# A local attention stage rewritten as one interleaved order of tiles on every engine

## The chip, the cores and the metric

The kernel runs on one core of a Trainium2 chip. The metric is the device time of one execution in microseconds; the time shown for a kernel is the median of its runs. The core has five engines that each work through their own program: TensorE (PE, with its weight loads as PEld), VectorE (DVE), ScalarE (ACT), GpSimd (POOL) and SyncE (SP), which here only issues transfers. They meet through semaphores: an instruction waits until a counter has reached a value, and another one counts it up when it is done.

## The reference, cut to what matters

A tensor x of 4 x 1024 tokens by 128 features is normalised. One branch is a small block attention (16 heads, blocks of 32). The other is two layers of local attention with a feed-forward part; the two are multiplied and added to x. The change touches the local attention only:

```
h = shift_token(x);  q, k, v = split(h @ wqkv, 3)          # 8 heads of 64
q = l2norm(q) * qs;  k = l2norm(k) * ksc
q, k = rotary_xpos(q, k)
# windows of 64 tokens; each sees its own window and the one before it
sim = einsum('bhwid,bhwjd->bhwij', q * 8, [k_prev_window, k_window])
sim = where(mask, -max, sim);  attn = softmax(sim)
out = einsum('bhwij,bhwjd->bhwid', attn, [v_prev_window, v_window])
x = x + out @ wo
```

## The kernel before

All 4096 tokens are kept in SBUF, features on partitions. The local stage of a layer (L = 0, 1) goes over 32 tiles of 128 tokens; `local(n, par)` is one step of it on each engine, and `steps` calls it for n in a row. After it comes the feed-forward part in 8 chunks of 512 tokens, and before the first stage the block attention.

For one tile m the work is this. TensorE projects q, k and v (three matmuls of 512 columns each, the input split into a high and a low half) into banks 0, 1 and 2 of PSUM. ScalarE squares q and k, VectorE sums the squares, and ScalarE makes inverse norms of them (Relu, Ln, Exp: `lognt`, `ss`). VectorE turns q by position (`tA`, `tB`, `qr`) and scales k (`kn`), GpSimd turns k (`kA`, `kB`, `kr`) and multiplies q by its inverse norm (line 1359). TensorE transposes qr and kr into bank 3, ScalarE copies them to `qT` and `kT`. Masks and scores go to banks 4 and 5 in two groups of heads; VectorE takes maxima (line 1130), ScalarE exponentials with their sums (line 880), VectorE the inverse sums, GpSimd multiplies the probabilities by them (line 1348). TensorE transposes the probabilities into bank 6, ScalarE copies them to `pT`. The values product (line 415, `ps<-pT,VB` and `ps<-pT,V`) goes to bank 7, ScalarE copies it to `oT`, the output product `ps<-oT,wo` goes to bank 3, and VectorE adds it to X.

A window also sees the one before it. So transfers on SP's queue carry the last 64 columns of `kT` into the other slot (line 376), and the halves of V, crosswise on partitions, into `VB` (lines 378 and 380). A third kind copies each finished tile of X, the second half of its features one token later, into `XS[1]` for the feed-forward part (lines 348 and 349). SP does this in a strict order, one `back(n, par)` a tile, and each transfer waits for its semaphores at its place. The wait on `xs_dma` at the head of `back` is for the XS copies issued by the step before to have landed; it keeps the counter exact.

The order on every engine is written out by hand in `local`. VectorE splits the input 512 tokens at a time, in every fourth step (`split_into`, lines 968 and 970). ScalarE copies V from bank 2 (line 849).

Of the kernel before, what the change touches and what calls it, by code (L numbers as in the profile page):

```python
# [32 lines left out]
P = 128  # L33
# [45 lines left out]
def build(nc, a, out):  # L79
    with ExitStack() as ctx:  # L80
# [52 lines left out]
        V = sb("V", [P, 2, INNER])  # L133
        VB = sb("VB", [P, 2, INNER])
        ss = sb("ss", [P, 2, 2 * HEADS])
# [99 lines left out]
        l_qk = sem("l_qk")  # L235
        l_v = sem("l_v")
        l_sq = sem("l_sq")
        l_qm = sem("l_qm")
        l_norm = sem("l_norm")
# [6 lines left out]
        l_qn = sem("l_qn")  # L246
        l_kr = sem("l_kr")
        l_tr = sem("l_tr")
        l_tre = sem("l_tre")
# [3 lines left out]
        l_score = sem("l_score")  # L253
        l_max = sem("l_max")
        l_exp = sem("l_exp")
        l_rinv = sem("l_rinv")
        l_prob = sem("l_prob")
        l_pT = sem("l_pT")
        l_pTe = sem("l_pTe")
# [48 lines left out]
        def _(sp):  # L308
# [49 lines left out]
            for L in range(DEPTH):  # L358
# [4 lines left out]

                def back(n, par):
                    nxt = 1 - par
                    base = L * TILES
                    turned, done = held(2 * (base + n + 1)), held(base + n + 1)
                    scored, pv1 = held(2 * (base + n)), held(base + n)
                    copied = held(xs_before_local(L) + 32 * (n - 2))
                    if live(n, -3, TILES):  # L370

                        sp.wait_ge(xs_dma, copied)
                    if live(n, 0, TILES):
                        sp.wait_ge(l_tre, turned)
                        wait(sp, l_score, scored)
                        sp.dma_start(kT[:, nxt, :, 0:WIN], kT[:, par, :, P:P + WIN]).then_inc(k_prev[nxt], 16)
                        sp.wait_ge(l_ve, done)
                        sp.dma_start(VB[64:P, par, :], V[0:64, par, :]).then_inc(v_prev[par], 16)
                        wait(sp, l_o, pv1)
                        sp.dma_start(VB[0:64, nxt, :], V[64:P, par, :]).then_inc(v_prev[nxt], 16)  # L380
                    if live(n, -2, TILES):
                        copy_shifted(XS[1], n - 2, P, x_before_local(L) + n - 1)

                if L == 0:

                    sp.wait_ge(zeros_made, 2)
                    sp.wait_ge(windows_zero, 1)
                    sp.dma_start(kT[:, 0, :, 0:WIN], kT[:, 1, :, P:P + WIN]).then_inc(k_prev[0], 16)
                    sp.dma_start(VB[0:64, 0, :], V[64:P, 1, :]).then_inc(v_prev[0], 16)
                steps(0, TILES + 1, back)  # L390
# [22 lines left out]
        def _(pe):  # L413
# [104 lines left out]
            def layer(L, tail):  # L518
# [6 lines left out]
                def project(c, hi, lo, made):  # L525

                    mm3(ps[:, c, :], hi, lo, wqkv[:, 0, c * INNER:(c + 1) * INNER],
                        wqkv[:, 1, c * INNER:(c + 1) * INNER]).then_inc(made, 1)

                def transposed(n, par, src, ready):  # L530
                    pe.wait_ge(ready, base + n + 1)
                    for c in range(4):
                        last = turn(ps[:, 3, c * P:(c + 1) * P], src[:, par, c * P:(c + 1) * P])
                    last.then_inc(l_tr, 1)

                def local(n, par):
                    nxt = 1 - par
                    now, ahead = [[split[:, (m // TPC) % 2, i, (m % TPC) * P:(m % TPC + 1) * P] for i in range(2)]
                                  for m in (n + 2, n + 1)]
                    if live(n, 2, TILES):  # L540
                        pe.wait_ge(l_split, L * CHUNKS + (n + 2) // TPC + 1)
                        wait(pe, l_qm, base + n + 2)
                        project(0, *now, l_qk)
                    if live(n, 0, TILES):

                        wait(pe, x_new, (x_before_local(L) + n - 2) if not isinstance(n, int) or n > 2 else 0)
                        transposed(n, par, qr, l_qn)

                    def scores():
                        if live(n, 0, TILES):  # L550
                            pe.wait_ge(l_tre, 2 * (base + n + 1))

                            pe.wait_ge(k_prev[par], 16 * ((base + n) // 2 + 1))
                            wait(pe, l_exp, 8 * (base + n))

                            first = 1 if par else live_mask(n)
                            half = [slice(64 * i, 64 * i + 64) for i in range(2)]
                            for w, grp in ((0, 0), (1, 1), (1, 0), (0, 1)):
                                kind = 1 if w else first
                                mm(ps[half[w], 4 + grp, :], ident_bf[half[grp], half[grp]],  # L560
                                   lmask[half[grp], bass.ds(kind * CHUNK, CHUNK)], True, False)
                            for s in range(4):
                                for w, grp in ((0, 0), (1, 1), (1, 0), (0, 1)):
                                    last = mm(ps[half[w], 4 + grp, s * P:(s + 1) * P],
                                              qT[half[grp], par, s, half[w]],
# [893 lines left out]
```

## Time and profile before

| | |
|---|---|
| median of 3 runs | 907.86 us (907.16 to 908.72) |
| profiled execution | 909.96 us, its span 908.2 us |
| TensorE busy | 800.1 us (88%) |
| VectorE busy | 664.4 us (73%) |
| ScalarE busy | 654.3 us (72%) |
| GpSimd busy | 523.9 us (58%) |
| chain that ended last | PE 56%, ACT 17%, DVE 16%, issue 7% |
| transfers | 48.24 MB, under 512 B 40410 of 64704 packets |

The span is the time from the first to the last instruction of the profiled execution. Busy time counts only working instructions, so an engine that waits on a semaphore is not busy. The chain goes back from the last instruction, at each step to what released it; it passes through an engine also where that engine waits for others in turn. Times within the span are microseconds from its start. The "granted clock" is the part of TensorE's full clock that it got: 1.00 is 2.4 GHz, 0.50 is 1.2 GHz.

### The profile page before, as it was taken

What the parts mean: (1) busy time and instruction counts of PE and PEld (TensorE: products, weight loads), DVE (VectorE), ACT (ScalarE), POOL (GpSimd) and SP (SyncE); (2) the same over time, 40 slices, a digit from 0 to 9 for tenths busy, and PEclk for the clock granted to TensorE, in tenths of its full rate; (3) what the DMA queues carried; (4) which work ended last, traced back from release to release, by engine and by line L of the source; (5) the groups of instructions that cost most, each with busy time, mean ns of one, the idle gap of its engine ahead of it and who ended that gap; (6) DMA issues with size and microseconds to landing.
All of it is one profiled execution on the core that took longest, in us unless ns stands there. A gap on an engine that the chain in (4) does not pass through costs nothing.

```text
span 908.2 us, 26049 instructions
## 1 busy us (share of the span) xinstructions
PE 800.1 (88%) x9848; PEld 610.5 (67%) x9848; DVE 664.4 (73%) x1347; ACT 654.3 (72%) x2053; POOL 523.9 (58%) x521
## 2 busy tenths in 40 slices
PE   4779999779999999999989887999999999988985
PEld 1458778557777778777756545777877777775652
DVE  1577998677887787877457767778787788745765
ACT  2337777479899899889743337989988998974463
POOL 0363333078888888888511017888888888951100
PEclk8899999889999999999999998999999999999997
DMA  9110001012222222222201121222222222222001
GB/s 308 44 45 3 4 4 41 3 47 55 57 57 63 55 58 55 60 57 63 51 18 24 29 63 37 64 53 58 57 61 56 62 52 58 58 51 100 1 36 58
DMA packets 64704, 48.24 MB, mean 53 GB/s; under 512 B 40410, under 2 KB 50948, under 8 KB 64068
## 3 DMA queue, kind: packets, MB, share of 16 engines
q1 hardware_dynamic: 64580, 46.57, 19.9%
q8 instruction: 80, 1.31, 0.6%
q14 instruction: 44, 0.36, 0.1%
HBM read 10.63 MB, written 2.10 MB: 14 GB/s over the span
## 4 chain that ended last, share of the span: by engine, by line
PE 56%; ACT 17%; DVE 16%; issue 7%; POOL 1%; DMA 1%; SPq 1%; DVEq 0%; ACTq 0%; POOLq 0%
PE ps L415 47%; PE ps L425 9%; ACT prob L880 6%; DVE nmax L1130 3%; ACT sq L822 3%; DVE nt L1158 2%; ACT V L849 2%; ACT oT L831 2%; DVE split L970 2%; ACT kT L856 1%; ACT pT L826 1%; DVE prob L1217 1%; DVE split L968 1%; DMA awo<-in_awo 1%; ACT qT L841 1%
## 5 line engine op out<-in xcount | busy, mean ns | idle before, releaser
L880 ACT ACTIVATE prob<-ps,nmax 128x128 f32<-128x128 f32 x512 | 181.8, 374 | 36.7 <-DVE nmax L1130 36.7
L415 PE MATMUL ps<-wqkv,split 128*128 128x512 f32 x576 | 188.2, 438 | 14.2 <-DVE split L970 10.1
L1348 POOL TENSOR_TENSOR prob<-prob,rinv 128x512 f32<-128x512 f32 x128 | 133.9, 1046 | 88.4 <-DVE rinv L1116 45.8
L415 PEld LDWEIGHTS ps<-wqkv,split 128*128 128x128 f32 x576 | 97.5, 195 | 33.5 <-DVE split L970 10.2
L1130 DVE TENSOR_REDUCE nmax<-ps 128x4 f32<-128x512 f32 x128 | 83.6, 686 | 48.3 <-PE ps L415 48.3
L425 PE MATMUL ps<-ident,prob 128*128 128x128 f32 x640 | 98.3, 276 | 13.9 <-POOL prob L1348 13.1
L880 ACT ACTIVATION_READ_ACCUMULATOR prob<-ps,nmax 128x1 f32 x512 | 109.0, 213 | 0.0
L1359 POOL TENSOR_TENSOR qr<-qr,ss 128x512 f32<-128x512 f32 x64 | 66.9, 1046 | 53.7 <-DVE qr L1142 53.7
L425 PEld LDWEIGHTS ps<-ident,prob 128*128 128x128 f32 x640 | 76.2, 142 | 28.3 <-POOL prob L1348 17.4
L415 PE MATMUL ps<-oT,wo 128*128 128x128 f32 x512 | 73.9, 287 | 22.0 <-ACT oT L831 22.0
L826 ACT ACTIVATE pT<-ps 128x512 f32<-128x512 f32 x128 | 80.0, 625 | 10.7 <-PE ps L425 9.1
L415 PE MATMUL ps<-split,w 128*128 128x512 f32 (+1 forms) x288 | 81.4, 427 | 6.6 <-DVE prob L1217 6.3
L415 PEld LDWEIGHTS ps<-oT,wo 128*128 128x128 f32 x512 | 62.1, 191 | 37.3 <-ACT oT L831 36.3
L822 ACT ACTIVATE sq<-ps 128x512 f32<-128x512 f32 x128 | 81.8, 640 | 5.1 <-PE ps L415 5.0
L1370 POOL TENSOR_TENSOR kr<-kA,kB 128x512 f32<-128x512 f32 x64 | 82.4, 1287 | 5.0
L1364 POOL TENSOR_TENSOR kA<-kn,lrot 128x512 f32<-128x512 f32 x64 | 81.8, 1278 | 0.0
L1313 POOL TENSOR_TENSOR qr<-ident,rstd 128x512 f32<-128x512 f32 x16 | 16.6, 1042 | 99.1 <-DVE rstd L962 96.0
L415 PEld LDWEIGHTS ps<-split,w 128*128 128x128 f32 (+1 forms) x288 | 50.4, 180 | 31.1 <-DVE prob L1217 10.1
L1330 POOL TENSOR_TENSOR prob<-D,hmask 128x512 f32<-128x512 f32 x32 | 35.1, 1097 | 59.5 <-PE ps L415 59.4
L1142 DVE TENSOR_TENSOR qr<-tA,tB 128x512 f32<-128x512 f32 x64 | 68.6, 1072 | 0.0
L415 PE MATMUL ps<-pT,VB 128*64 128x64 f32 x1024 | 66.3, 228 | 1.5 <-issue 1.5
L415 PE MATMUL ps<-kT,qT 64*64 64x128 f32 x2048 | 66.8, 269 | 0.0
(139 smaller groups left out, 1871.9 us busy)
## 6 DMA issues: line engine op xcount, KB each, us to landing
VB<-V SPq DMA_DIRECT2D x129, 128.0 KB, 2.4
kT<-kT SPq DMA_DIRECT2D x65, 128.0 KB, 2.4
XS<-X SPq DMA_DIRECT2D x32, 128.0 KB, 2.3
XS<-X SPq DMA_DIRECT2D x128, 32.0 KB, 1.9
D<-in_xT SPq DMA_DIRECT2D x8, 256.0 KB, 4.4
XS<-in_xT SPq DMA_DIRECT2D x2, 1024.0 KB, 6.7
out_T<-XS SPq DMA_DIRECT2D x8, 256.0 KB, 2.0
raw<-in_wqkv SPq DMA_DIRECT2D x2, 768.0 KB, 4.4
```

Source lines behind the costliest of these rows:

```text
L415: return nc.tensor.matmul(o, l, r, start=start, stop=stop, skip_group_check=True)
L425: return nc.tensor.matmul(o, i, ident[:], is_transpose=True, start=True, stop=True, skip_group_check=True)
L822: nc.scalar.activation(sq[:, c, :], ps[:, c, :], ACT.Square).then_inc(l_sq, 1)
L826: nc.scalar.activation(pT[:, grp, :], ps[:, 6, :], ACT.Copy).then_inc(l_pTe, 1)
L880: nc.scalar.activation(prob[:, par, grp, s * P:(s + 1) * P], ps[:, 4 + grp, s * P:(s + 1) * P], ACT.Exp, bias=nmax[:, par, grp * 4 + s:grp ...
L1130: v.tensor_reduce(nmax[:, par, 4 * grp:4 * grp + 4], ps[:, 4 + grp, :].rearrange("p (s k) -> p s k", s=4), AX_X, ALU.max, negate=True).the ...
L1142: v.tensor_tensor(qr[:, nxt, :], tA[:], tB[:], ALU.add).then_inc(l_qr, 1)
L1330: g.tensor_tensor(kexp[:, par, :].rearrange("p (b h k) -> p b h k", b=BLKS, h=INGRP), part(kR, n, P).rearrange("p (b k) -> p b k", b=BLKS) ...
L1348: g.tensor_tensor(p4, p4, rinv[:, slot, 4 * grp:4 * grp + 4].unsqueeze(2).broadcast_to([P, 4, P]), ALU.mult).then_inc(l_prob, 1)
L1359: g.tensor_tensor(hd(qr[:, nxt, :]), hd(qr[:, nxt, :]), ss[:, nxt, 0:8].unsqueeze(2).broadcast_to([P, HEADS, HD]), ALU.mult).then_inc(l_qn, 1)
L1364: g.tensor_tensor(hd(kA[:]), hd(kn[:]), row8(2, pos, 0, HD), ALU.mult)
L1370: g.tensor_tensor(kr[:, nxt, :], kA[:], kB[:], ALU.add).then_inc(l_kr, 1)
```

## The change

- The local stage is cut into small functions, one for each operation on a tile, and every engine calls them in a written order in which one step works on tiles from n+4 or n+5 down to n-3. TensorE now does the scores of tile n, the values of tile n-2 and the output of tile n-3 in one step; it did the values of n-1 and the output of n-2.
- Semaphores are split: one for q and one for k, and one for each group of heads.
- q is no longer multiplied by its inverse norm on GpSimd. The exponential takes the inverse norm as its scale, a column of `ss`, and the maxima (now `rawmax`) are multiplied by it in two small VectorE operations a tile.
- The split of the input goes from VectorE, 512 tokens at a time, to GpSimd, 128 tokens at a time (`input_high`, `input_low`).
- V is copied out of PSUM by VectorE instead of ScalarE, and has three slots instead of two.
- On SP, the X tile that is copied to XS in a step is that of n-4, it was n-2; the rest of `back` has its old form.

```diff
-        V = sb("V", [P, 2, INNER])
+        V = sb("V", [P, 3, INNER])
...
                 def back(n, par):
-                    nxt = 1 - par
-                    base = L * TILES
-                    turned, done = held(2 * (base + n + 1)), held(base + n + 1)
-                    scored, pv1 = held(2 * (base + n)), held(base + n)
-                    copied = held(xs_before_local(L) + 32 * (n - 2))
-                    if live(n, -3, TILES):
-
-                        sp.wait_ge(xs_dma, copied)
+                    nxt, done = 1 - par, base + n + 1
+                    if live(n, -5, TILES):
+                        sp.wait_ge(xs_dma, xs_before_local(L) + 32 * (n - 4))
                     if live(n, 0, TILES):
-                        sp.wait_ge(l_tre, turned)
-                        wait(sp, l_score, scored)
+                        sp.wait_ge(l_tk, done)
+                        wait(sp, l_score[1], done - 1)
                         sp.dma_start(kT[:, nxt, :, 0:WIN], kT[:, par, :, P:P + WIN]).then_inc(k_prev[nxt], 16)
                         sp.wait_ge(l_ve, done)
-                        sp.dma_start(VB[64:P, par, :], V[0:64, par, :]).then_inc(v_prev[par], 16)
-                        wait(sp, l_o, pv1)
-                        sp.dma_start(VB[0:64, nxt, :], V[64:P, par, :]).then_inc(v_prev[nxt], 16)
-                    if live(n, -2, TILES):
-                        copy_shifted(XS[1], n - 2, P, x_before_local(L) + n - 1)
+                        sp.dma_start(VB[64:P, par, :], V[0:64, done % 3, :]).then_inc(v_prev[par], 16)
+                        wait(sp, l_o, done - 1)
+                        sp.dma_start(VB[0:64, nxt, :], V[64:P, done % 3, :]).then_inc(v_prev[nxt], 16)
+                    if live(n, -4, TILES):
+                        copy_shifted(XS[1], n - 4, P, x_before_local(L) + n - 3)
...
-                steps(0, TILES + 1, back)
+                steps(0, TILES + 3, back)
...
+                def scores(m):
...
+                        pe.wait_ge(l_tq, base + m + 1)
+                        pe.wait_ge(l_tk, base + m + 1)
+
+                        pe.wait_ge(k_prev[m % 2], 16 * ((base + m) // 2 + 1))
...
+                def values_summed(m):
...
+                        wait(pe, l_oe, base + m)
+                        pe.wait_ge(l_pTe[0], base + m + 1)
+                        pe.wait_ge(l_pTe[1], base + m + 1)
+                        pe.wait_ge(l_ve, base + m + 1)
+                        pe.wait_ge(v_prev[m % 2], 32 * ((base + m) // 2 + 1))
...
+                def local(n, par):
+                    q_projected(n + 3)
+                    scores(n)
+                    probs_turned(n - 2, 1)
+                    k_turned(n + 1)
+                    v_projected(n)
+                    values_summed(n - 2)
+                    output(n - 3)
+                    k_projected(n + 3)
+                    probs_turned(n - 1, 0)
+                    q_turned(n + 2)
...
+                def exponentials(m, grp):
+                    if 0 <= m < TILES:
+                        act.wait_ge(l_max[grp], base + m + 1)
+                        for s in range(4):
+                            col = slice(grp * 4 + s, grp * 4 + s + 1)
+                            nc.scalar.activation(prob[:, m % 2, grp, s * P:(s + 1) * P],
+                                                 ps[:, 4 + grp, s * P:(s + 1) * P], ACT.Exp, bias=nmax[:, m % 2, col],
+                                                 scale=ss[:, (base + m) % 3, 2 * s + grp:2 * s + grp + 1],
+                                                 accum_out=rsum[:, m % 2, col]).then_inc(l_exp[grp], 1)
+
+                def local(n, par):
+                    exponentials(n, 1)
+                    exponentials(n, 0)
+                    probs_copied(n - 1, 0)
+                    k_squared(n + 3)
+                    q_copied(n + 2)
+                    q_squared(n + 4)
+                    o_copied(n - 2)
+                    norm_floor(n + 3)
+                    probs_copied(n - 1, 1)
+                    norm_log(n + 3)
+                    k_copied(n + 2)
+                    norm_inverse(n + 3)
...
+                def v_copied(m):
+                    if 0 <= m < TILES:
+                        dve.wait_ge(l_v, base + m + 1)
+                        wait(dve, l_o, base + m - 2)
+                        if base + m >= 2:
+                            dve.wait_ge(v_prev[m % 2], 32 * ((base + m - 2) // 2 + 1))
+                        v.tensor_copy(V[:, (base + m + 1) % 3, :], ps[:, 2, :]).then_inc(l_ve, 1)
...
+                def scaled_maxima(m, grp):
+                    if 0 <= m < TILES:
+                        dve.wait_ge(l_rawmax[grp], base + m + 1)
+                        v.tensor_tensor(nmax[:, m % 2, 4 * grp:4 * grp + 4], rawmax[:, m % 2, 4 * grp:4 * grp + 4],
+                                        ss[:, (base + m) % 3, grp:HEADS:2], ALU.mult).then_inc(l_max[grp], 1)
...
+                    maxima(n, 1)
+                    q_cos(n + 3)
+                    scaled_maxima(n, 1)
+                    maxima(n, 0)
+                    k_scaled(n + 2)
+                    scaled_maxima(n, 0)
+                    q_sin(n + 3)
+                    added_to_x(n - 3)
+                    v_copied(n)
+                    q_summed(n + 3)
+                    inverse_sums(n, 1)
+                    inverse_sums(n, 0)
+                    q_rotated(n + 3)
+                    k_summed(n + 3)
...
-                        g.tensor_tensor(hd(qr[:, nxt, :]), hd(qr[:, nxt, :]),
-                                        ss[:, nxt, 0:8].unsqueeze(2).broadcast_to([P, HEADS, HD]),
-                                        ALU.mult).then_inc(l_qn, 1)
...
                 def local(n, par):
...
+                    input_low(n + 4)
+                    k_sin(n + 2)
+                    k_cos(n + 2)
+                    k_rotated(n + 2)
+                    normalised(n, 1)
+                    input_high(n + 5)
+                    normalised(n, 0)
```

On TensorE, in the middle of the first local stage, from the masks of one tile on, before. `lmask` are the masks, `kT,qT` the scores, `oT,wo` the output product, `pT,VB` and `pT,V` the values, `wqkv,split` a projection, `ident,...` a set of four transposes.

```order
L415 MATMUL ps<-lmask,ident_bf 64x512 x4
L415 MATMUL ps<-kT,qT 64x128 x16
L415 MATMUL ps<-oT,wo 128x128 x4
L415 MATMUL ps<-pT,VB 64x64 x2
L415 MATMUL ps<-pT,V 64x64 x2
```

And of the changed kernel, from the end of the values of one step to those of the next.

```order
L418 MATMUL ps<-pT,V 64x64 x2
L418 MATMUL ps<-oT,wo 128x128 x4
L418 MATMUL ps<-wqkv,split 128x512 x3
L428 MATMUL ps<-ident,prob 128x128 x4
L428 MATMUL ps<-ident,qr 128x128 x4
L418 MATMUL ps<-wqkv,split 128x512 x3
L418 MATMUL ps<-lmask,ident_bf 64x512 x4
L418 MATMUL ps<-kT,qT 64x128 x16
L428 MATMUL ps<-ident,prob 128x128 x4
L428 MATMUL ps<-ident,kr 128x128 x4
L418 MATMUL ps<-wqkv,split 128x512 x3
L418 MATMUL ps<-pT,VB 64x64 x2
```

The values stood behind the output product, right after the scores; they now stand behind two sets of transposes and V's projection, and belong to tile n-2. The output product follows them.

On SP, the transfers of one tile with their waits, before: the kT window, the two halves of VB, the two halves of XS, and the next kT window.

```order
L376 DMA kT<-kT 128x4x64 [waits l_score,l_tre,xs_dma]
L378 DMA VB<-V 64x512 [waits l_ve]
L380 DMA VB<-V 64x512 [waits l_o]
L348 DMA XS<-X 64x128 [waits x_new]
L349 DMA XS<-X 64x128
L376 DMA kT<-kT 128x4x64 [waits l_score,l_tre,xs_dma]
```

And in the changed kernel.

```order
L379 DMA kT<-kT 128x4x64 [waits l_score1,l_tk,xs_dma]
L381 DMA VB<-V 64x512 [waits l_ve]
L383 DMA VB<-V 64x512 [waits l_o]
L354 DMA XS<-X 64x128 [waits x_new]
L355 DMA XS<-X 64x128
L379 DMA kT<-kT 128x4x64 [waits l_score1,l_tk,xs_dma]
```

The places of the transfers are the same; the waits have new names, and XS takes the tile four back instead of two. `l_o` still counts the values of the tile before the one whose kT window was sent last.

## Rows read from the trace of the kernel before

**Rows 1.** Table by stage, second local stage: us, busy time (count) of each engine.
```profile
549.30:806.60 257.30, 233.62 (x3077) 190.05 (x3080) 199.36 (x375) 231.42 (x829) 214.00 (x215) 0.99 0.24 57
```

**Rows 2.** Timeline, TensorE, scores of first and last tiles: start, us, engine, line, out<-in.
```profile
188.78 0.41 PE L415 MATMUL ps<-lmask,ident_bf 64*64 64x512 bf16 x4
...
445.08 0.41 PE L415 MATMUL ps<-lmask,ident_bf 64*64 64x512 bf16 x4
...
446.33 1.16 PE L415 MATMUL ps<-oT,wo 128*128 128x128 f32 x8
...
549.27 0.53 PE L415 MATMUL ps<-lmask,ident_bf 64*64 64x512 bf16 x4
...
806.55 0.41 PE L415 MATMUL ps<-lmask,ident_bf 64*64 64x512 bf16 x4
```

**Rows 3.** Timeline, TensorE, inside one tile.
```profile
341.51 0.34 PE L415 MATMUL ps<-pT,VB 128*64 128x64 f32 x4
...
342.59 0.97 PE L415 MATMUL ps<-wqkv,split 128*128 128x512 f32 x3
...
343.39 0.60 PE L425 MATMUL ps<-ident,qr 128*128 128x128 f32 x4
...
343.83 0.60 PE L425 MATMUL ps<-ident,prob 128*128 128x128 f32 x4
...
344.18 0.94 PE L415 MATMUL ps<-wqkv,split 128*128 128x512 f32 x3
```

**Rows 4.** Timeline, SP's queue of transfers, same tile.
```profile
342.70 0.46 SPq L380 DMA_DIRECT2D VB<-V  x1
...
343.84 0.60 SPq L349 DMA_DIRECT2D XS<-X  x1
347.14 0.63 SPq L376 DMA_DIRECT2D kT<-kT  x1
```

**Rows 5.** Groups of instructions: shapes, count | busy us, mean ns | idle before.
```profile
L849 ACT ACTIVATE V<-ps 128x512 f32<-128x512 f32 x64 | 41.4, 647 | 0.0
...
L1359 POOL TENSOR_TENSOR qr<-qr,ss 128x512 f32<-128x512 f32 x64 | 66.9, 1046 | 53.7 <-DVE qr L1142 53.7
...
L970 DVE TENSOR_TENSOR split<-XS,split 128x512 fp32r<-128x512 f32 x16 | 23.5, 1470 | 0.6
...
L869 ACT ACTIVATE lognt<-lognt,floor 128x16 f32<-128x16 f32 x64 | 19.0, 297 | 0.3
...
L968 DVE CAST split<-XS 128x512 fp32r<-128x512 f32 x16 | 10.2, 635 | 0.0
...
L876 ACT ACTIVATE ss<-lognt 128x16 f32<-128x16 f32 x64 | 14.3, 223 | 0.1
...
L1170 DVE RECIPROCAL rinv<-rsum 128x4 f32<-128x4 f32 x64 | 11.2, 176 | 25.0 <-ACT prob L880 25.0
```

**Rows 6.** DMA issues: first and last kT copy of 62: count, KB, us to landing.
```profile
kT<-kT SPq DMA_DIRECT2D x1, 128.0 KB, 3.8
...
kT<-kT SPq DMA_DIRECT2D x1, 128.0 KB, 3.3
```

**Rows 7.** Tile XS, 250 to 400 us, its 18 pairs of copies.
```profile
DMA to landing us min/median/max: 1.7/1.9/3.3
```

**Rows 8.** Stretches, TensorE: us, busy (count), granted clock, DMA share, GB/s.
```profile
168.60:170.50 1.90, 0.04 (x1) 1.00 0.00 0
170.70:174.10 3.40, 3.40 (x12) 0.50 0.00 0
...
552.00:559.70 7.70, 5.34 (x87) 1.00 0.09 21
559.70:561.70 2.00, 0.01 (x1) 1.00 0.57 131
563.30:566.60 3.30, 3.11 (x12) 0.50 0.00 0
```

**Rows 9.** Timeline, TensorE, a projection at the lower clock.
```profile
195.92 1.63 PE L415 MATMUL ps<-wqkv,split 128*128 128x512 f32 x3
```

More of the change, by code:

```diff
@@ L536, in local @@
[L536 to L557, printed above, removed]
-                            for w, grp in ((0, 0), (1, 1), (1, 0), (0, 1)):
[L559 to L565, printed above, removed]
-                                              kT[half[grp], par, s, 64 * w:64 * w + P], False, True)
-                                    if s == 3 and w != grp:
-                                        last.then_inc(l_score, 1)
-                    def turned_probs(grp):
-                        if live(n, -1, TILES):
-                            pe.wait_ge(l_prob, 2 * (base + n - 1) + grp + 1)
-                            wait(pe, l_pTe, 2 * (base + n - 1) + grp)
-                            for s in range(4):
-                                last = turn(ps[:, 6, s * P:(s + 1) * P], prob[:, nxt, grp, s * P:(s + 1) * P])
-                            last.then_inc(l_pT, 1)
-                    def output():
-                        if not live(n, 0, TILES):
-                            pe.wait_ge(x_new, x_before_local(L) + n - 2)
-                        pe.wait_ge(l_oe, base + n - 1)
-                        if live(n, 0, TILES):
-                            pe.wait_ge(l_tre, 2 * (base + n + 1))
@@ new lines, in probs_turned, with output @@
+                def probs_turned(m, grp):
+                    if 0 <= m < TILES:
+                        pe.wait_ge(l_prob[grp], base + m + 1)
+                        wait(pe, l_pTe[1 - grp], base + m + grp)
+                        for s in range(4):
+                            last = turn(ps[:, 6, s * P:(s + 1) * P], prob[:, m % 2, grp, s * P:(s + 1) * P])
+                        last.then_inc(l_pT[grp], 1)
+                def output(m):
+                    if 0 <= m < TILES:
+                        if m == 0:
+                            pe.wait_ge(wo_in, 16 * (L + 1))
+                        pe.wait_ge(l_oe, base + m + 1)
+                        if 0 <= m + 4 < TILES:
+                            pe.wait_ge(l_tk, base + m + 4 + 1)
+                        elif 0 <= m + 4 < TILES:
+                            pe.wait_ge(l_tq, base + m + 4 + 1)
+                        elif 0 <= m - 1 < TILES:
+                            pe.wait_ge(x_new, x_before_local(L) + m - 1 + 1)
@@ L682, in layer @@
                 local(TILES, 0)
+                bias_products()
+                local(TILES + 1, 1)
+                local(TILES + 2, 0)
                 variance(2, 2, 0)
@@ L1176, in layer @@
                 if L == 0:
                     dve.wait_ge(xs_dma, xs_before_local(0))
-                    local(-3, 1)
                     a_tile(TILES - 1, 1)
-                    local(-2, 0)
-                    local(-1, 1)
+                    steps(-3, -1, local)
                     dve.wait_ge(a_done, TILES)
@@ L1185, in layer @@
                     dve.wait_ge(xs_dma, xs_before_ffn(L - 1) + 32)
+                    steps(-3, -4, local)
+                    tail(CHUNKS, 0)
                     local(-3, 1)
-                    tail(CHUNKS, 0)
                     local(-2, 0)
@@ L1260, in layer @@
                 ffn_bias(L)
-                add_to_x(TILES - 2)
+                local(TILES + 1, 1)
                 def scaled(j, t):
@@ L1378, in _ @@
+                steps(-5, TILES - 1 + 0, local)
+                pool.wait_ge(l_trq, base + TILES)
                 nb = L * CHUNKS
```

457 lines of the change are left out of this document (243 added, 214 removed).

## The prediction

> **What bounds the kernel now.** I read the table by stage first. One local stage (scores of tile 0 to scores of tile 31) is 257.3 us, in which TensorE is busy 233.6, ScalarE 231.4, GpSimd 214.0 and VectorE 199.4 [rows 1]. Over 31 intervals that is 7.54, 7.47, 6.90 and 6.43 us a tile, against 8.30 that pass. No engine is full, two are close. Second, the timeline of TensorE. The scores of tile 0 start at 188.78 and 549.27, those of tile 31 at 445.08 and 806.55 [rows 2], so the two stages take 256.3 and 257.3 us, 513.6 together, 8.28 a tile. Within one tile the pieces, start to next start, are [rows 2, 3]: masks and scores 1.25 (445.08 to 446.33), values 1.08 (341.51 to 342.59), a projection 0.80 (342.59 to 343.39), a set of four transposes 0.44 (343.39 to 343.83) or 0.35 (343.83 to 344.18), and the output product about 1.1, by its 1.16 whose tail lies under the next. A tile has three projections and four sets of transposes (0.35 twice, 0.40 for k, 0.44): 1.25 + 1.1 + 1.08 + 2.40 + 1.54 = 7.4. The 0.9 us between 7.4 and 8.28 is what a better order could give back. Third, the queue of transfers on SP. Each tile issues, strictly in turn, the copy of kT's window, two halves of VB, and two halves of the shifted residual XS. Today it follows at leisure: after the values of a tile end, near 342.59, the second half of VB goes out at 342.70, the second half of XS at 343.84, and the next kT copy at 347.14 [rows 3, 4]. The scores that read this kT copy start a whole tile later, so nothing waits for it.
>
> **The change part by part.**
>
> V's copy leaves ScalarE, 0.65 us a tile, and becomes a VectorE copy. GpSimd's scaling of q goes, 1.05 a tile. VectorE's split, 1.47 + 0.64 for four tiles, is 0.53 a tile and goes to GpSimd in eighths of that work: two operations on 128 columns, each between 0 and the 1.05 of a 512-column operation, together some 0.9. VectorE gains two products on 128x4, near 0.2 each by its smallest rows [rows 5]. Busy times a tile become: ScalarE 7.47 - 0.65 = 6.8, VectorE 6.43 - 0.53 + 0.65 + 0.4 = 6.95, GpSimd 6.90 - 1.05 + 0.9 = 6.75 (5.9 to 8.0), TensorE unchanged.
>
> The exponential now reads its scale from a column. Nearest rows: a 16-column activation with no column operand is 223 ns, one with a column for its bias 297 [rows 5]. I take the difference, 0.07, for each of eight exponentials: 0.6 a tile (0 to 0.6). ScalarE is then 7.4. The Trainium skill, ScalarE: Activation LUTs, section What ACT_TABLE_LOAD costs, gives about 93 ns for each column operand, 0.74 a tile, and ScalarE 7.6; the trace agrees within 20 ns. It would matter only in the fast rival below.
>
> The order on TensorE is what I price highest. In step n it did scores(n), output(n-2), values(n-1). Now it does scores(n), transposes of probabilities(n-2), transposes of k(n+1), V's projection(n), values(n-2), and only then output, k's projection, two sets of transposes, q's projection and scores(n+1). SP's program kept its form. For the scores of tile n+1 it must issue in order: the second VB half, which waits for values(n-2); XS of tile n-5 in two halves; then, after a wait for exactly these two XS copies to land, the kT copy that scores(n+1) waits for. Before, the same entry waited for values that TensorE had done one whole step earlier. Now they are done inside the step. This closes a loop through two landings: scores(n) start, values(n-2) end, VB, XS, XS landed, kT, kT landed, scores(n+1) start.
>
> Its length: scores 1.25, transposes 0.35 and 0.40, a projection 0.80, values 1.08, together 3.88 on TensorE [rows 2, 3]. To the VB issue 0.11 (342.59 to 342.70). To the second XS issue 1.14 (342.70 to 343.84) [rows 4]. To its landing 1.9, median, up to 3.3 [rows 7]; the kT issue at 347.14 is 3.3 after 343.84, so today's queue already shows this wait once. kT's landing: 37 of the 62 copies of both stages take 2.3 to 2.5, the others 3.0 to 4.6, mean 2.8; first and last stand in [rows 6]. Hand-overs 0.1. Sum 3.88 + 0.11 + 1.14 + 1.9 + 2.8 + 0.1 = 9.93 us a tile. In the 6.05 us from the end of the values TensorE has 1.1 + 0.80 + 0.35 + 0.44 + 0.80 = 3.5 of other work, so it stands idle 2.6 (2.0 where kT lands in 2.3).
>
> The skill's page DMA: Bandwidth & Descriptors, section Anatomy of one DMA, fits a transfer as 2.0 us and its bytes at 436 GB/s. By that kT's 128 KB take 2.3 and an XS half of 32 KB takes 2.1; the loop would be 9.6 always. The trace has the same 2.3 for the usual kT copy but 3 to 4.6 for two in five, and the measurement decides.
>
> For which tiles: the XS copies start with step 4 of SP and the wait for them with step 5, so scores(1) to (5) are free of the loop (the chain without XS is 0.11 + 0.5 + 2.8, about 3.4, against 3.5 of work), and scores(6) to (31) are in it: 26 intervals a stage. For the five free ones I take 8.0, between 7.4 and 8.28.
>
> The clock adds to it. Where TensorE stood idle about 2 us, the granted clock afterwards fell to half (1.2 GHz instead of 2.4) for 3.4 us: idle 168.6 to 170.5, half until 174.1; idle 559.7 to 561.7, half from 563.3 to 566.6 [rows 8]. From the first to the last of these there are five such gaps at full clock, and four were followed by it; after the one at 552.0 the clock held at 1.00 until 559.7 [rows 8]. A projection at half clock shows 1.63 where the usual one is 0.97 [rows 3, 9], so 3.4 us at half clock do the work of 2.0 and lose 1.4. The loop leaves a gap of 2.0 or more before each scores, and the slow stretch would follow on the 3.88 that are in the loop. I take 0.8 x 1.4 = 1.1 a tile (0 to 1.7, the whole stretch doubled): 9.9 + 1.1 = 11.0.
>
> Start and end of a stage: one more step to fill and drain, V's projection 0.80, values 1.08, output 1.1, so 3.0 a stage (0 to 6), 6 in all. The XS copies of the last tiles leave later, but the feed-forward part reads its last chunk many steps on.
>
> Sum: stages 2 x (5 x 8.0 + 26 x 11.0) = 652 against 513.6, plus 138.4; fill and drain 6. The profiled execution took 909.96 (span 908.2, with 1.8 around it); 909.96 + 144.4 = 1054.4. The median of the runs shown is 2.1 below the profiled one, so 1052.
>
> **Rivals.**
>
> Clock holds (A). The loop is there but the clock stays full, as after 552.0. 9.9 a tile: 2 x (40 + 257.4) = 594.8, plus 81.2 and 6, less 2.1: 995. With landings always the shortest (1.9 and 2.3) the loop is 9.4: 969. For it: one gap in five. Against it: four in five, and gaps that come every tile.
>
> The wait for XS costs nothing (B), say because these copies are counted as landed from an earlier step. The kT copy then goes right behind the second XS issue: 3.88 + 0.11 + 1.14 + 0.64 + 2.8 + 0.1 = 8.7, which is 2 x (40 + 226) = 532, and 934 in the end. Against it: the count waited for is that of tile n-5, issued one entry before.
>
> The queue is no bound (C), the side of faster. It holds if the kT copy for scores(n+1) is out before values(n-2) end. Then the tile is the fullest engine, TensorE 7.54 with a little waiting, 7.6, and the split's stall on every fourth tile is gone: 62 x 7.6 = 471, minus 42.4, plus 6, so 871. This is the place where it turns: once the chain from the end of the values to the landing of kT is under 3.5 us, nothing of the queue is seen. It is 6.05 by the rows, nearly double.
>
> GpSimd at its upper bound of 8.0 a tile would hide behind the loop and changes nothing.
>
> **How the numbers follow.** Loop with the clock falling in most tiles 0.62 (own range 1020 to 1090: 11.6 a tile gives 1083); A 0.26; B 0.06; C 0.06. Predicted time 1052. The range leaves out C and B and the rim: 975 to 1090. A measurement of this kernel tells 0.2% from nothing. Faster 0.05 (C), same 0.01, slower 0.94.
>
> **What would show it.** After: SP's waits name TensorE before the second VB half, then XS, in front of the kT issue, in every tile from the fifth or sixth; TensorE idle 2 to 3 us right before the masks of each tile; masks to masks 10 to 11.5 us, but near 8 for the first five tiles; the granted clock at half for 3.4 us in most tiles; busy shares of ScalarE and GpSimd down to about 65%. I am wrong if the kT issue stands in the trace well before the end of the values, or if masks follow each other in under 9 us; wrong only on the clock if the gaps are there and it stays at full speed.

## The result, and the profile after

The changed kernel takes 1054.5 us, median of 4 runs (1048.6 to 1062.1), beside 907.5 us for the kernel before (4 runs, 907.1 to 908.7). The ratio is 1.162, with a 95% interval of 1.155 to 1.170. The profiled execution took 1054.97 us, span 1053.2.

First the page of the changed kernel: busy time of each engine, TensorE's granted clock in 40 slices, and the chain that ended last by engine.

```profile
PE 836.6 (79%) x9848; PEld 639.5 (61%) x9848; DVE 701.7 (67%) x1507; ACT 660.6 (63%) x1989; POOL 524.0 (50%) x585
...
PEclk7999998799999999987899989999889999989998
...
PE 43%; ACT 25%; issue 17%; DVE 8%; DMA 3%; POOL 2%; SPq 1%; DVEq 0%; POOLq 0%; ACTq 0%
```

Every engine has a smaller share than before, and "issue", the time in which an engine waited for nothing that the profile can name, has gone from 7% to 17% of the chain. So no engine is busier than it was, and none has become the bound by its own work. The groups say where the new idle time lies: masks, exponential, the sum of q's two halves, the maxima (line, engine, shapes, count | busy us, mean ns | idle before, and who ended it).

```profile
L910 ACT ACTIVATE prob<-ps,nmax,ss 128x128 f32<-128x128 f32 x512 | 226.4, 476 | 0.5 <-DVE nmax L1210 0.5
...
L1203 DVE TENSOR_REDUCE rawmax<-ps 128x4 f32<-128x512 f32 x128 | 87.9, 687 | 148.7 <-PE ps L418 148.7
...
L418 PE MATMUL ps<-lmask,ident_bf 64*64 64x512 bf16 x256 | 30.5, 459 | 139.5 <-issue 120.7
...
L1178 DVE TENSOR_TENSOR qr<-tA,tB 128x512 f32<-128x512 f32 x64 | 96.3, 1505 | 0.0
```

TensorE stands still for 139.5 us in front of the masks, the first matmuls of a tile's scores, and VectorE for 148.7 us in front of the maxima, which read these scores. All else in the stage waits for the scores. The table by stage (us, then busy time and count of TensorE, its weight loads, VectorE, ScalarE, GpSimd, the granted clock, the transfers' share and GB/s) puts it beside [rows 1]:

```profile
192.80:509.10 316.30, 243.65 (x3020) 198.09 (x3021) 216.26 (x451) 230.66 (x790) 209.49 (x236) 0.92 0.19 45
625.60:942.70 317.10, 244.99 (x3017) 199.53 (x3016) 216.52 (x452) 231.84 (x794) 212.30 (x240) 0.92 0.19 45
```

The scores of the first and the last tile of each stage, to be read beside [rows 2]:

```profile
192.76 0.64 PE L418 MATMUL ps<-lmask,ident_bf 64*64 64x512 bf16 x4 [1.89 <-DMA kT<-kT]
...
509.08 0.58 PE L418 MATMUL ps<-lmask,ident_bf 64*64 64x512 bf16 x4 [2.42 <-issue]
...
625.57 0.41 PE L418 MATMUL ps<-lmask,ident_bf 64*64 64x512 bf16 x4
...
942.75 0.64 PE L418 MATMUL ps<-lmask,ident_bf 64*64 64x512 bf16 x4 [2.85 <-issue]
```

The stages take 316.3 and 317.2 us, 633.5 together, where they took 513.6: 119.9 of the 145.0 us that the profiled execution is longer. A stage lasts 316 instead of 257 us with nearly the same work, and the clock is 0.92 instead of 0.99. Per tile VectorE is busy 6.98, ScalarE 7.44, GpSimd 6.76 us (a stage over 31); the prediction had 6.95, 7.4 and 6.75. These sums came out as worked; the added time is not in them.

It is in one loop. Here are two tiles in a row, SP's queue first, then the masks and, of the second tile, the output product behind the values on TensorE (start, us, engine, line, out<-in), to be read beside [rows 3, 4].

```profile
347.89 0.46 SPq L383 DMA_DIRECT2D VB<-V  x1
348.39 0.96 SPq L354 DMA_DIRECT2D XS<-X  x1
349.40 0.60 SPq L355 DMA_DIRECT2D XS<-X  x1
351.31 0.63 SPq L379 DMA_DIRECT2D kT<-kT  x1
...
358.02 0.46 SPq L383 DMA_DIRECT2D VB<-V  x1
358.52 0.60 SPq L354 DMA_DIRECT2D XS<-X  x1
359.16 0.60 SPq L355 DMA_DIRECT2D XS<-X  x1
361.06 0.63 SPq L379 DMA_DIRECT2D kT<-kT  x1
```
```profile
342.37 0.64 PE L418 MATMUL ps<-lmask,ident_bf 64*64 64x512 bf16 x4 [2.64 <-issue]
...
353.90 0.41 PE L418 MATMUL ps<-lmask,ident_bf 64*64 64x512 bf16 x4 [2.69 <-issue]
...
357.90 1.16 PE L418 MATMUL ps<-oT,wo 128*128 128x128 f32 x8
...
363.58 0.41 PE L418 MATMUL ps<-lmask,ident_bf 64*64 64x512 bf16 x4 [2.25 <-issue]
```

Follow one turn. Masks at 353.90; values end near 357.9, the second VB half is issued at 358.02, 4.12 us after the masks; the second XS half 1.14 later, at 359.16; the kT copy 1.90 later, at 361.06, when XS has landed; the next masks 2.52 later, at 363.58, when kT has landed. Sum 9.68. Of the turn before, which began at the lower clock (the masks took 0.64 where 0.41 is usual), the same four pieces are 5.52, 1.51, 1.91 and 2.59, sum 11.53. SP's own waits between 250 and 450 us (line, for whom: us in total, times, longest) name both ends of the loop:

```profile
SPq L383 <- PE ps L418: 110.7, 19, 7.0
SPq L379 <- DMA XS<-X: 25.4, 19, 2.9
```

In the kernel before, between 250 and 400 us, the wait for XS cost SP 1.4 us in 2 cases:

```profile
SPq L376 <- DMA XS<-X: 1.4, 2, 0.8
```

I divided each of the 52 looped turns (26 a stage) at the same four starts (us):

| masks to masks, piece | predicted | most turns | mean, stage 1 | mean, stage 2 |
|---|---|---|---|---|
| masks to second VB half | 3.99 + clock 1.1 | 4.12 | 4.83 | 4.93 |
| to second XS half | 1.14 | 1.14 | 1.21 | 1.20 |
| to the kT copy | 1.9 | 1.91 | 2.06 | 1.97 |
| to the next masks | 2.9 | 2.57 | 2.57 | 2.60 |
| sum | 11.0 | 9.74 | 10.67 | 10.69 |

### The profile page after: what moved, and what is told of

It reads as the page before. It is cut to its first block, busy times and chain, and to the rows that moved or that the text cites. A ratio compares the mean times of both kernels' runs of the same rounds, so it can differ in the third digit from the quotient of the medians.

```text
span 1053.2 us, 26733 instructions
## 1 busy us (share of the span) xinstructions
PE 836.6 (79%) x9848; PEld 639.5 (61%) x9848; DVE 701.7 (67%) x1507; ACT 660.6 (63%) x1989; POOL 524.0 (50%) x585
## 4 chain that ended last, share of the span: by engine, by line
PE 43%; ACT 25%; issue 17%; DVE 8%; DMA 3%; POOL 2%; SPq 1%; DVEq 0%; POOLq 0%; ACTq 0%
PE ps L418 35%; ACT prob L910 14%; PE ps L428 8%; ACT qT L866 3%; ACT pT L879 2%; ACT kT L872 2%; ACT sq L861 2%; DMA kT<-kT 2%; ACT lognt L896 1%; DMA XS<-X 1%; DVE prob L1281 1%; DMA awo<-in_awo 1%; DVE vexp L1084 1%; ACT ss L903 1%; POOL kA L1439 0%
## 5 line engine op out<-in xcount | busy, mean ns | idle before, releaser
L910 ACT ACTIVATE prob<-ps,nmax,ss 128x128 f32<-128x128 f32 x512 | 226.4, 476 | 0.5 <-DVE nmax L1210 0.5
L418 PE MATMUL ps<-wqkv,split 128*128 128x512 f32 x576 | 192.0, 444 | 19.5 <-DVE kn L1196 14.3
L1203 DVE TENSOR_REDUCE rawmax<-ps 128x4 f32<-128x512 f32 x128 | 87.9, 687 | 148.7 <-PE ps L418 148.7
L1432 POOL TENSOR_TENSOR prob<-prob,rinv 128x512 f32<-128x512 f32 x128 | 154.9, 1213 | 38.6 <-DVE rinv L1216 38.6
L1445 POOL TENSOR_TENSOR kB<-kn,lrot 128x256 f32<-128x256 f32 x64 | 46.6, 728 | 221.7 <-DVE kn L1196 221.7
L418 PE MATMUL ps<-lmask,ident_bf 64*64 64x512 bf16 x256 | 30.5, 459 | 139.5 <-issue 120.7
L910 ACT ACTIVATION_READ_ACCUMULATOR prob<-ps,nmax,ss 128x1 f32 x512 | 115.3, 225 | 0.0
L1178 DVE TENSOR_TENSOR qr<-tA,tB 128x512 f32<-128x512 f32 x64 | 96.3, 1505 | 0.0
L418 PE MATMUL ps<-kT,qT 64*64 64x128 f32 x2048 | 88.5, 322 | 0.0
L418 PEld LDWEIGHTS ps<-kT,qT 64*64 64x64 f32 x2048 | 80.5, 164 | 5.0 <-issue 2.6
L418 PEld LDWEIGHTS ps<-pT,VB 128*64 128x64 f32 x1024 | 53.5, 139 | 28.5 <-issue 28.5
```

The lines of the kernel that those rows point to most:

```text
L418: return nc.tensor.matmul(o, l, r, start=start, stop=stop, skip_group_check=True)
L910: nc.scalar.activation(prob[:, m % 2, grp, s * P:(s + 1) * P], ps[:, 4 + grp, s * P:(s + 1) * P], ACT.Exp, bias=nmax[:, m % 2, col], scale ...
L1178: v.tensor_tensor(qr[:, m % 2, :], tA[:], tB[:], ALU.add).then_inc(l_qr, 1)
L1203: v.tensor_reduce(rawmax[:, m % 2, 4 * grp:4 * grp + 4], ps[:, 4 + grp, :].rearrange("p (s k) -> p s k", s=4), AX_X, ALU.max, negate=True) ...
L1432: g.tensor_tensor(p4, p4, rinv[:, m % 2, 4 * grp:4 * grp + 4].unsqueeze(2).broadcast_to([P, 4, P]), ALU.mult).then_inc(l_prob[grp], 1)
L1445: g.tensor_tensor(hd(kB[:])[:, :, 0:32], hd(kn[:])[:, :, 32:64], row8(3, m, 0, 32), ALU.mult)
```

## The experiments

The ratios are against the kernel before, run on the same chip beside each kernel (908.5 to 908.7 us). Counts and stage lengths are those of each kernel's profiled execution. Two theories stood against each other at first. The loop theory: the time is the circle through the two landings, with the clock on top. Its rival: the new order on the engines is itself slower, and the queue only shows it. Experiments 1 and 2 decide between them.

**1. The kT copy one entry earlier.** It leaves SP ahead of the second VB half that waits for the values; tile 0's goes out before the first step.

```diff
+                    if live(n, 1, TILES):
+                        sp.wait_ge(l_tk, done + 1)
+                        wait(sp, l_score[1], done)
+                        sp.dma_start(kT[:, par, :, 0:WIN], kT[:, nxt, :, P:P + WIN]).then_inc(k_prev[par], 16)
                     if live(n, 0, TILES):
-                        sp.wait_ge(l_tk, done)
-                        wait(sp, l_score[1], done - 1)
-                        sp.dma_start(kT[:, nxt, :, 0:WIN], kT[:, par, :, P:P + WIN]).then_inc(k_prev[nxt], 16)
                         sp.wait_ge(l_ve, done)
```

> SP's copy of kT's window is issued one entry earlier, so it no longer stands behind the VB half and the XS copies that follow the values of tile n-2. Theory (a loop of scores, values, VB, XS, landing, kT, landing): the loop is open, TensorE waits for nothing on SP, masks to masks 7.6 to 8.3 us, no lower clock in the stage, 880 to 915 us. Rival (the new order itself is too tight: the exponential with a scale column at 476 ns instead of 374, q's sum at 1505 ns instead of 1072): the stage stays over 9.5 us a tile and the time over 1000.

Measured: 890.8 us, ratio 0.980 (0.978 to 0.983). One transfer moved by one place takes back 164 us. Stage table, SP's waits between 250 and 420 us of it, and three masks in a row:

```profile
194.10:427.50 233.40, 225.71 (x3020) 182.51 (x3024) 207.36 (x450) 226.14 (x790) 207.69 (x236) 0.99 0.26 61
```
```profile
SPq L384 <- PE ps L422: 68.3, 23, 3.4
SPq L379 <- DMA XS<-X: 27.3, 22, 2.0
```
```profile
299.38 0.41 PE L422 MATMUL ps<-lmask,ident_bf 64*64 64x512 bf16 x4
...
307.12 0.41 PE L422 MATMUL ps<-lmask,ident_bf 64*64 64x512 bf16 x4
...
314.57 0.41 PE L422 MATMUL ps<-lmask,ident_bf 64*64 64x512 bf16 x4
```

The tiles follow each other in 7.74 and 7.45, 7.54 in the mean, TensorE has no gap before the masks, and the clock is back at 0.99. SP still waits for the XS landing in every tile, 22 times in 170 us, 1.24 us each, nearly as long as the 1.34 in the changed kernel (25.4 in 19), but nothing urgent stands behind it. The rival falls: in the same order of work each stage is 22 to 23 us shorter than in the kernel before.

**2. The XS copies in front of the second VB half.** The kT copy stays where the change has it; its wait for XS is met early, and only the landing of kT is left behind the values.

```diff
+                    if live(n, -4, TILES):
+                        copy_shifted(XS[1], n - 4, P, x_before_local(L) + n - 3)
+                    if live(n, 0, TILES):
                         wait(sp, l_o, done - 1)
                         sp.dma_start(VB[0:64, nxt, :], V[64:P, done % 3, :]).then_inc(v_prev[nxt], 16)
-                    if live(n, -4, TILES):
-                        copy_shifted(XS[1], n - 4, P, x_before_local(L) + n - 3)
```

> Only the XS copies move, in front of the VB half that waits for the values; kT stays behind that half. Theory: XS issue and landing (1.24 + 1.9 us) leave the loop, which keeps 3.9 + 0.1 + 0.5 + kT's landing 2.3 to 4.6 + 0.1 = 6.9 to 9.2 us; with 7.4 of work on TensorE 7.6 to 8.6 a tile, 890 to 935 us. Rival (XS's landing costs nothing, it is only kT's place): hardly changed, over 1000.

Measured: 895.5 us, ratio 0.986 (0.983 to 0.988), 7.56 and 7.60 us a tile in the looped turns. With the 3.05 of XS (two issues and a landing) off the path, the chain behind the values is VB's issue and kT's landing, an estimate of 3.1 (0.5 and 2.57), and TensorE has 3.5 of other work to put there. So it takes both landings, in a row, to make the bound: taking away either is enough.

**3. TensorE kept busy in the gap.** Eight matmuls of 512 columns, whose result is not used, ahead of the wait for the kT copy, from tile 6 on. They write the bank of the scores, so that wait also moves behind the two waits for the exponentials.

```diff
-
-                        pe.wait_ge(k_prev[m % 2], 16 * ((base + m) // 2 + 1))
                         wait(pe, l_exp[0], 4 * (base + m))
                         wait(pe, l_exp[1], 4 * (base + m))
+                        if 6 <= m:
+                            for _ in range(8):
+                                mm(ps[:, 4, :], wqkv[:, 0, 0:P], wqkv[:, 0, 0:INNER])
+
+                        pe.wait_ge(k_prev[m % 2], 16 * ((base + m) // 2 + 1))
```

> From tile 6 on, eight matmuls of 512 columns, about 2 us, fill the gap in front of the scores; their product is thrown away and all else is as in the changed kernel. Theory (part of the loss is the lower clock after the gap): the granted clock stays near 1.00 in the stages, every tile takes the 9.7 us of the tiles at full clock, 980 to 1005 us in spite of more work. Rival (the clock is no part of it): 1050 or more.

Measured: 1024.5 us, ratio 1.126 (1.123 to 1.129); a miss, above the range. The granted clock did what was wanted (table of a stretch in the first stage; 0.99 in the second too):

```profile
220.00:500.00 280.00, 257.45 (x3050) 209.31 (x3047) 199.03 (x411) 211.91 (x724) 189.66 (x214) 0.99 0.20 47
```

More work on TensorE made the kernel 30 us faster. Divided as above, masks to VB is 4.12 or 4.13 again in 48 of 52 turns (mean 4.20 and 4.25 instead of 4.83 and 4.93): this part of the loss, 0.66 a tile, was the clock. I had expected each turn at 9.7, and the mean is 10.12, which over 52 turns makes 22 us, the size of the miss. Most of what lies above a full-clock turn is a thing of its own: the piece from the kT issue to the masks is 2.42 in most turns but over 3 in 12 of them (up to 4.33), mean 2.70, so 0.28 a tile. These are late landings of kT, which the changed kernel hardly has; see the last section. The lower clock is left in 3 turns (0.1 a tile).

**4. The queue made longer.** Two more transfers (2 KB each, into a scratch tile) between the second VB half and XS.

```diff
                         sp.dma_start(VB[0:64, nxt, :], V[64:P, done % 3, :]).then_inc(v_prev[nxt], 16)
+                        for i in range(2):
+                            wait(sp, extra[i], 16 * (done - 1))
+                            sp.dma_start(scr[:, i, :], pmask[:]).then_inc(extra[i], 16)
```

> Two more small transfers are issued on SP between the second VB half and the XS copies, some 1.3 us of issue time. Theory: they lie in the loop, 52 tiles x 1.3 = 68 us more, and a longer gap with a lower clock after it more often: 1110 to 1150 us. Rival (SP is not in the loop, its waits only follow TensorE's): 1050 to 1060.

Measured: 1198.4 us, ratio 1.319 (1.316 to 1.322), a miss, 48 us above the range. SP's queue, one turn, and the table of a stretch:

```profile
317.88 0.46 SPq L385 DMA_DIRECT2D VB<-V  x1
318.39 1.25 SPq L388 DMA_DIRECT2D scr<-pmask  x2
...
320.32 0.60 SPq L357 DMA_DIRECT2D XS<-X  x1
322.50 0.63 SPq L381 DMA_DIRECT2D kT<-kT  x1
```
```profile
345.00:500.00 155.00, 109.69 (x1139) 89.42 (x1138) 78.37 (x172) 90.18 (x302) 83.13 (x96) 0.78 0.17 37
```

From the second VB half to the second XS half now pass 2.44 instead of 1.14: 1.30 for two issues. A turn that runs at full clock is longer by about that, 11.05. The mean turn is 13.39, though, because the piece from the masks to VB went from a mean of 4.9 to 6.3 (most of them 6.6 to 6.7), at a clock of 0.78. The median gap before the masks is 3.6 here (2.3 in the changed kernel), and after 48 of the 50 gaps over 3.5 us the next turn was slow. So a microsecond of queue cost more than itself once TensorE starved: 1.30 added became 2.7, 141 us over 52 turns. The expectation had 68 us for the issues and left at most 28 for the clock.

**5. The earlier kT copy, and another order at the end of the stage.** On VectorE the feed-forward weights, sets of statistics, a centring and a scaling go ahead of the last steps of the local stage, on TensorE one variance and one normalisation too, about where the kernel before had them.

```diff
                 local(TILES - 1, 1)
-                local(TILES, 0)
                 ffn_weights(L)
                 links(0, 1, NEWTON, 0, 2)
                 centre(nb, 2, shifted(XS[1], 2, CHUNK), 2)
+                local(TILES, 0)
...
-                local(TILES + 2, 0)
                 links(2, 1, 6, 2)
                 scaled(0, tA)
                 links(2, 7, 9, 2)
+                local(TILES + 2, 0)
...
-                local(TILES + 2, 0)
                 variance(2, 2, 0)
                 pe.wait_ge(ln_rstd, rstd_before(L, 0) + 1)
                 norm_bcast(0, 0, nb, 0)
+                local(TILES + 2, 0)
```

> As the run with kT early, and at the end of a stage VectorE prepares the feed-forward weights and the first inverse deviations before it waits for the output of tile 29, and TensorE broadcasts the first norm before the last output product, as in the kernel before. Theory (the stage's end grew by 9 to 13 us, since this work stood behind a 4.3 us wait of VectorE and ran into a lower clock): 4 to 8 us less a stage, 875 to 883 us. Rival (the end is longer because there is one more step to drain): within 3 us of 890.8.

Measured: 883.7 us, median of 5 runs (880.3 to 886.4), ratio 0.973 (0.971 to 0.975): the fastest of all, 7.1 us under experiment 1 and just above the expected range. VectorE in the last steps of the first stage, of experiment 1 and then of this one (last masks at 427.45 and 424.49):

```profile
439.06 0.29 DVE L1227 TENSOR_TENSOR X<-X,ps 128x128 f32<-128x128 f32 x1 [4.33 <-PE ps L422]
439.26 0.57 DVE L1134 TENSOR_SCALAR w<-raw,vecs 128x682 fp32r<-128x682 f32 x1
```
```profile
429.49 0.29 DVE L1227 TENSOR_TENSOR X<-X,ps 128x128 f32<-128x128 f32 x1 [1.92 <-PE ps L422]
431.68 0.55 DVE L1134 TENSOR_SCALAR w<-raw,vecs 128x682 fp32r<-128x682 f32 x1
```

In experiment 1 the weights stood behind an addition to X that waited 4.33 us, and came 11.8 us after the last masks; here they come 7.2 after them. Between the stages and after the second the profiled execution is 5.6 and 3.3 us shorter than that of experiment 1. These 9 us are read from one execution of each, and that of this kernel was its fastest. The several pieces moved were not tried one by one.

**6. V's copy back on ScalarE**, on top of experiment 1: the same function with an activation (Copy) in place of VectorE's copy, called behind the exponentials.

```diff
                     exponentials(n, 0)
+                    v_copied(n)
                     probs_copied(n - 1, 0)
```

> As the run with kT early, but V is again copied by ScalarE, right after its exponentials. Theory (with the loop open ScalarE is near the bound: eight exponentials at 0.44 and seven copies at 0.48 are 7.4 of 7.54 us): 0.3 to 0.5 us a tile more, 62 intervals, 908 to 922 us. Rival (TensorE alone is the bound and V's copy has room): 889 to 895 us.

Measured: 913.6 us, ratio 1.006 (1.004 to 1.008). The table of the first stage:

```profile
194.00:435.00 241.00, 225.13 (x3011) 181.28 (x3004) 188.89 (x416) 236.72 (x812) 205.44 (x234) 0.99 0.25 58
```

ScalarE is busy 236.7 of 241.0 us and the tile takes 7.91, every time. Without the loop V's copy on ScalarE, at this place in its order, costs 23 us: it makes the difference between the faster kernel of experiment 1 and one a little slower than before. In the changed kernel ScalarE waits for the scores, so there the move may be worth nothing; that pair was not run.

**7. Only the split per tile on GpSimd**, in the kernel before.

```diff
-                        split_into(j % 2, shifted(XS[0], j, CHUNK), CHUNK, l_split, L * CHUNKS + j)
...
+                    input_low(n + 4)
...
+                    input_high(n + 5)
```

> The kernel before with one part of the change alone: the input is split per tile on GpSimd. Theory (of the 8.27 us a tile of before, 0.34 are a stall of 1.4 on each fourth tile, and nothing else moves): all intervals 7.9, 888 to 895 us. Rival (GpSimd, 6.9 us busy of 7.9, gets 0.7 more and delays kr and the probabilities): 900 to 912 us.

Measured: 891.7 us, ratio 0.982 (0.981 to 0.984). Masks of the kernel before, then of this one:

```profile
329.43 0.41 PE L415 MATMUL ps<-lmask,ident_bf 64*64 64x512 bf16 x4
...
338.74 0.41 PE L415 MATMUL ps<-lmask,ident_bf 64*64 64x512 bf16 x4
...
346.67 0.41 PE L415 MATMUL ps<-lmask,ident_bf 64*64 64x512 bf16 x4
```
```profile
210.34 0.41 PE L415 MATMUL ps<-lmask,ident_bf 64*64 64x512 bf16 x4
...
218.40 0.41 PE L415 MATMUL ps<-lmask,ident_bf 64*64 64x512 bf16 x4
...
226.44 0.41 PE L415 MATMUL ps<-lmask,ident_bf 64*64 64x512 bf16 x4
```

Before, every fourth turn is 9.3 and the others 7.93; now all are near 8.03. The stall on the 512-token split was 1.37 every fourth tile; the others grew by 0.1, where I had expected nothing. Inside the stages this is 14.3 us of the 19.4 by which the profiled execution is shorter; the other 5.1 lie outside. This one part, in the old order, ends as fast as experiment 1 with the whole change (891.7 and 890.8), by another road. Here the stages take 499.3 and all outside them 389.5 us; there they take 468.5 and 421.8. The new order is 31 us better inside the stages and 32 us worse at their ends.

## Why the prediction came out right, and where it did not

It forecast 1052, and 1054.5 was measured. The bound it named is the one that experiments 1 and 2 took away and 4 made longer. That the number is within 3 us is luck, though: it is the sum of errors that cancel. The stages took 633.5 us where it had 652 (18.5 too many); the rest took 419.7 against 394.6 before, 25.1 more where it had 6 (19 too few).

- **The loop.** Which turns: the first five took 38.8 and 39.3 us (predicted 40), the sixth was already in the loop at 9.7 and 10.3. Its length was 9.74 in most turns, predicted 9.93. The landing of kT was mis-sized: I took the mean of the kernel before, 2.8 [rows 6], and a hand-over of 0.1; masks follow the issue by 2.57 here. Landings and issues that were late add 0.2 to the mean in other places. The Trainium skill, DMA: Bandwidth & Descriptors, section Anatomy of one DMA, would have given an estimate of 9.6 for the turn by its 2.0 us and bytes at 436 GB/s. The section has this fit for transfers that GpSimd issues, which the prediction didn't say; the ones here are issued by SP. All the same 59 of 65 kT copies landed within 2.5 here, against 2.3 by the fit, so for kT's landing the fit was nearer than my mean of 2.8.
- **The clock.** The mechanism is right (experiment 3: 0.66 a tile came back with the clock), the size is not. "I take 0.8 x 1.4 = 1.1 a tile" rested on four gaps of five. Of 52 turns, 21 were lengthened (masks to VB over 5.4), six of these by 2.6 to 2.8, the others by 1.3 to 1.6; in the mean 0.76 a tile. Frequency too high (0.8 for 0.4), price too low (1.4 for 1.9). Over 52 turns that is 18 us, as much as the whole error of the stages; the shorter loop (-10) and the late landings (+10) cancel.
- **Start and end of a stage.** "3.0 a stage" counted TensorE's added work. Measured +4.0 before the first scores, +12.3 between the stages, +8.8 after the second: some 12.5 a stage. Of all terms this one failed most. The traces say where the time is, here behind the second stage (last masks at 806.55 and 942.75): the last addition to X and the first matmuls of the feed-forward part, before and after.

```profile
820.89 0.28 DVE L1122 TENSOR_TENSOR X<-X,ps 128x128 f32<-128x128 f32 x1
...
823.40 3.06 PE L415 MATMUL ps<-split,w 128*128 128x512 f32 x12
```
```profile
962.89 0.29 DVE L1223 TENSOR_TENSOR X<-X,ps 128x128 f32<-128x128 f32 x1 [1.63 <-PE ps L418]
...
968.26 3.05 PE L418 MATMUL ps<-split,w 128*128 128x512 f32 x12
```

  From the last masks to the last addition pass 20.1 us, before 14.3, and from there to the feed-forward part 5.4, before 2.5. So the end costs 8.7 a stage more, and the start the other 4; in the first stage the first masks waited 1.89 for their kT copy (192.76 above). The drain was priced by TensorE's own three pieces, and what shares an engine with it was left out: VectorE's weights for the feed-forward part waited behind additions to X. Experiment 5 takes back 9 us of the 27 that experiment 1 has there; the cause of the other 18 stays open.
- **The exponential with a column as scale.** 476 ns against 374: 0.10 each, predicted 0.07. With the 512-token split moved and no column it is 377 (experiment 7), in the seven kernels with the column 470 to 523. So it isn't the split; the column is the likely cause, but all seven have the new order too, and that order without a column was not run. The Trainium skill, ScalarE: Activation LUTs, section What ACT_TABLE_LOAD costs, gives about 93 ns, and the row of the changed kernel agrees within 10; in experiment 1 the difference is 138 (512). In the changed kernel ScalarE waits for the scores, so it should cost nothing there. In experiment 1 ScalarE, with 226 of 233 us, is as full as TensorE, so there it may count.
- **Rivals.** A (the clock holds) is what experiment 3 set up: with it the turn was still 10.1. B (the wait for XS costs nothing; its 934 us is 933 by its own terms) is refuted by SP's waits, 25.4 us in 19 cases, and by experiment 2. C gave 7.6 a tile and 871 us for a queue that doesn't bind; experiment 1 is that case, with 7.54 a tile as predicted and 890.8 in the end. Its missing 20 us are again the start and the ends of the stages.

## What to carry to other kernels

Where a queue issues in a fixed order, each wait in it holds everything behind it; moving work on an engine later by one step can close a circle through that queue though the queue's own program hasn't changed. Before reordering, write down for each transfer that the next step needs what is ahead of it in the queue, and add up the landings between the event that frees the first and the use of the last; in experiment 2 it was harmless at 3.1 us against 3.5 of other work, in the changed kernel 5.7 us (0.1, 1.14, 1.91 and 2.57) were not. And price the ends of a pipeline apart from its steady state: against experiment 7, a gain of 31 us inside was eaten by 32 at the ends.

## What the runs showed of the hardware

- **Late landings go with the moment of the copy, not with the transfer.** Of 65 kT copies of 128 KB, 28 took 3.0 us or more in the kernel before, 27 in experiment 1, 29 in 7; but 3 in the changed kernel and 1 in experiment 4, where TensorE stands idle during the landing. A busy TensorE alone does not do it: in experiment 2 it is as busy as in 1, and 2 kT copies were late. There 25 XS copies within the stages were late instead (none in experiment 1), all of them issued within 0.7 us of the start of a tile's masks. The halves of VB in experiment 1 say the same: of 50 issued near the masks (0.75 before to 1.1 us after) 24 were late, of the other 79 two. One of each, kT in experiment 1 (issued at 344.69, masks at 344.89) and XS in experiment 2 (issued at 344.44, masks at 344.54):

```profile
kT<-kT SPq DMA_DIRECT2D x1, 128.0 KB, 4.2
```
```profile
XS<-X SPq DMA_DIRECT2D x1, 32.0 KB, 3.7
```

  In experiment 3, 14 kT copies were late; there the eight added matmuls run during the landing. What in the engines' work at that moment delays a copy stays open.
- **The longer the gap, the surer the lower clock, in these two kernels.** Call a turn slow where masks to VB took over 5.4 us. In the changed kernel the turn after a gap of 2.2 to 2.6 us was slow in 11 of 37 cases, after 2.6 to 3.0 in 4 of 6, after more than 3.0 in 6 of 7; in experiment 4, after more than 3.5, in 48 of 50. All six turns that lost 2.6 to 2.8 us followed gaps of 2.99 or more. Within the shortest group the two outcomes show no pattern that I could find: the turns that begin at 241.25, 250.97 and 260.71 us have gaps of 2.24 to 2.31, the slow one at 270.48 has 2.33.

```profile
241.25 0.41 PE L418 MATMUL ps<-lmask,ident_bf 64*64 64x512 bf16 x4 [2.24 <-issue]
...
270.48 0.64 PE L418 MATMUL ps<-lmask,ident_bf 64*64 64x512 bf16 x4 [2.33 <-issue]
```

- **The same VectorE addition of two SBUF tiles takes very different times.** The sum of q's halves, 128x512, has a mean of 758 ns in experiment 6, 1072 before, 1152 in experiment 1, 1505 in the changed kernel and 1541 in experiment 3, with the same instruction; its place against the other engines' work differs between them. In the changed kernel it takes 0.43 us longer than before, in a stage where VectorE waits for the scores anyway. No run tested what makes it slow.
